# An RWKV layer with a SwiGLU block: how the receptance of chunk 1 and the keys of chunk 2 are mixed, and who makes the low parts of chunk 0

## What is computed

```python
xx = jnp.pad(x, ((0, 0), (1, 0), (0, 0)))[:, :-1]          # the step before
xk = x * time_mix_k + xx * (1.0 - time_mix_k)              # the same for xv, xr
k = jnp.einsum('btc,dc->btd', xk, Wk)                      # v and r with xv, xr
w = -jnp.exp(time_decay)
rwkv = jax.nn.sigmoid(r) * _wkv(w, time_first, k, v)
# one step of _wkv, with carries aa, bb, pp:
ww = u + kt; q = jnp.maximum(pp, ww); e1 = jnp.exp(pp - q); e2 = jnp.exp(ww - q)
y = (e1 * aa + e2 * vt) / (e1 * bb + e2)
ww2 = pp + w; q2 = jnp.maximum(ww2, kt); e1 = jnp.exp(ww2 - q2); e2 = jnp.exp(kt - q2)
aa, bb, pp = e1 * aa + e2 * vt, e1 * bb + e2, q2
# the layer:
x1 = _layernorm(x + jnp.einsum('btc,dc->btd', rwkv, Wo))
h = jax.nn.silu(x1 @ wg.T) * (x1 @ wu.T)
out = _layernorm(x1 + h @ wd.T)
```

## Time and profile before

| | us |
|---|---|
| median of 3 runs | 291.11 (290.76 to 291.33) |
| profiled execution, its time | 291.55 |
| profiled execution, span | 289.7 |
| PE busy | 273.9 (95% of the span) |
| DVE busy | 261.1 (90%) |
| ACT busy | 214.9 (74%) |
| POOL busy | 191.6 (66%) |

### The profile page before, as it was taken

One profiled execution on the slowest core, in us unless ns is written; L12 is line 12 of the kernel. 1 busy time (PEld: TensorE's weight loads), 2 busy tenths in 40 slices (PEclk: granted clock), 3 DMA queues, 4 the chain that ended last, 5 costly groups with the idle time before them and its releaser, 6 DMA issues.

```text
span 289.7 us, 4280 instructions
## 1 busy us (share of the span) xinstructions
PE 273.9 (95%) x1258; PEld 199.1 (69%) x1258; DVE 261.1 (90%) x451; ACT 214.9 (74%) x388; POOL 191.6 (66%) x155
## 2 busy tenths in 40 slices
PE   7999978889999999999999999999999999999990
PEld 5754565646794689648885679568965789778890
DVE  4996599899999999999999999999899999889773
ACT  3488797489667987699966986798858892799473
POOL 3638699979968875986768675986566580334051
PEclk9999999999999999999999999999999999999998
DMA  7900600220103102230204010210211020102003
GB/s 236 374 6 12 209 1 0 73 72 3 36 2 80 67 0 72 47 100 0 72 5 144 1 54 19 72 36 0 72 29 44 1 75 0 36 2 74 0 3 113
DMA packets 13541, 16.26 MB, mean 56 GB/s; under 512 B 720, under 2 KB 11216, under 8 KB 13520
## 3 DMA queue, kind: packets, MB, share of 16 engines
q1 hardware_dynamic: 12832, 15.48, 16.7%
q10 hardware_dynamic: 688, 0.53, 0.6%
HBM read 11.81 MB, written 4.19 MB: 55 GB/s over the span
## 4 chain that ended last, share of the span: by engine, by line
PE 72%; DVE 11%; ACT 8%; issue 4%; DMA 1%; POOL 1%; SPq 0%; DVEq 0%; POOLq 0%; ACTq 0%
PE bank_b L1163 12%; PE bank_a L1163 12%; PE bank_a L1186 11%; PE bank_b L1119 9%; PE bank_a L1082 7%; PE bank_c L1082 7%; PE bank_d L1082 7%; PE bank_b L1140 2%; DMA wkT<-wk 1%; DVE rwkv L786 1%; DVE state L746 1%; ACT L606 1%; POOL hlo L405 1%; PE bank_d L1109 1%; ACT wts L492 1%
## 5 line engine op out<-in xcount | busy, mean ns | idle before, releaser
L405 POOL TENSOR_TENSOR hlo<-hid,hhi 128x512 fp32r<-128x512 f32 (+1 forms) x37 | 54.0, 1466 | 31.7 <-ACT hhi L584 31.6
L378 POOL TENSOR_SCALAR wts<-gap,par 128x512 f32<-128x512 f32 (+1 forms) x18 | 35.9, 1995 | 24.4 <-DVE gap L714 23.5
L500 ACT ACTIVATE mix<-dx,par 128x512 f32<-128x512 f32 x48 | 31.4, 712 | 19.0 <-POOL dx L358 19.0
L1186 PE MATMUL bank_a<-wd_r,hhi 128*128 128x256 f32 x180 | 44.2, 287 | 1.0 <-POOL hlo L405 0.9
L1186 PE MATMUL bank_a<-wd_r,hlo 128*128 128x256 f32 x180 | 42.8, 279 | 0.0
L364 POOL TENSOR_TENSOR mix<-mix,xt 128x512 f32<-128x512 f32 (+1 forms) x36 | 40.7, 1164 | 0.3 <-ACT mix L500 0.3
L1186 PEld LDWEIGHTS bank_a<-wd_r,hhi 128*128 128x128 f32 x180 | 33.8, 188 | 3.5 <-issue 2.6
L1186 PEld LDWEIGHTS bank_a<-wd_r,hlo 128*128 128x128 f32 x180 | 33.8, 188 | 0.3 <-issue 0.2
L862 DVE TENSOR_TENSOR hid<-bank_b,act 128x512 f32<-128x512 f32 (+1 forms) x48 | 30.8, 643 | 3.6 <-issue 1.1
L584 ACT ACTIVATE hhi<-hid 128x512 fp32r<-128x512 f32 (+1 forms) x53 | 30.6, 579 | 4.4 <-DVE hid L862 4.4
L492 ACT ACTIVATE wts<-wts 128x512 f32<-128x512 f32 (+1 forms) x54 | 27.9, 577 | 7.5 <-DVE wts L723 7.3
(11 more groups left out here) (129 smaller groups left out, 598.1 us busy)
## 6 DMA issues: line engine op xcount, KB each, us to landing
xrow<-x SPq DMA_DIRECT2D x7, 512.0 KB, 3.8
xt<-xT SPq DMA_DIRECT2D x6, 513.0 KB, 3.7
out<-y_buf SPq DMA_DIRECT2D x6, 512.0 KB, 2.9
wg_i<-wg SPq DMA_DIRECT2D x1, 768.0 KB, 7.7
wu_i<-wu SPq DMA_DIRECT2D x1, 768.0 KB, 9.1
wd_i<-wd SPq DMA_DIRECT2D x1, 768.0 KB, 10.7
out<-y_buf SPq DMA_DIRECT2D x3, 256.0 KB, 2.2
xt<-xT SPq DMA_DIRECT2D x2, 257.0 KB, 2.9
```

The source lines that it names most:

```text
L378: nc.gpsimd.tensor_scalar(wts[:, OUT, h, 0:n], gap[:, h, 0:n], par[:, FIRST, h:h + 1], CAP, ALU.add, ALU.min).then_inc(out_arg_ready, 1)
L405: nc.gpsimd.tensor_tensor(hlo[:, m, 0:n], hid[:, m % NH, 0:n], hhi[:, m, 0:n].bitcast(f32), ALU.subtract).then_inc(hlo_ready, 1)
L500: nc.scalar.activation(mix[:, s, i, h, 0:n], dx[:, h, 0:n], ACT.Copy, scale=par[:, MIX + i, h:h + 1]).then_inc(dx_scaled, 1)
L1186: mm = nc.tensor.matmul(ffn[:, q, :], hp.bitcast(f32) if full else hp, w[:, m, :], start=(m == 0 and q % 2 == 0 and part is hhi), stop=(m ...
```

## The change

What it does, in the order of the program:

- ScalarE: the two range checks of the gate weights go ahead of an exponential and of `log_den(0)`. The by-product goes to `res2`, since `y`'s buffer now holds x of chunk 2. The scaling for R(1) is gone, and the one for K(2).
- SyncE: x of chunk 2 goes into `y`'s buffer and is loaded at once; x of chunk 3 goes to `xt` and waits for `mix_r1`; x of chunk 4 is loaded after chunk 3's mixes and stands behind the residual rows.
- VectorE: two new operations a half each, `mix_r1` (R of chunk 1, behind `x1_low(0)`) and `mix_k2` (K of chunk 2, behind `divide` of chunk 1). All of the denominator's scans of chunk 1 stand behind `mix_r1`. Low parts 4 and 5 of chunk 0 are gone.
- GpSimd: chunk 2's differences wait for `mix_r1`; half 0 of V(2) is mixed ahead of the `den` sums of chunk 1, half 1 behind them; all six low parts of chunk 0 follow in a row; the differences of chunk 3 wait for `mix_k2` and for the scaling of R(2).
- TensorE: `project_last_step(R)` is gone and R(1) is projected from its mix; the sum of the range flag stands between the halves of V(1); V(2)'s second half stands behind the whole of `down(0)`.

The diff, cut to its core:

```diff
             def load_xt(c):
-                if isinstance(c, int) and c == 2:
+                if isinstance(c, int) and c == 3:
                     sp.wait_ge(last_steps_done, 1)
-                elif isinstance(c, int) and c == 3:
-                    sp.wait_ge(squares_ready, 6)
-                elif isinstance(c, int) and c == 4:
-                    sp.wait_ge(mixed, 3 * CH)
-                elif not (isinstance(c, int) and c == 1):
+                    sp.wait_ge(r1_mixed, CH)
+                elif not (isinstance(c, int) and c < 3):
                     sp.wait_ge(mixed, (c - 2) * (3 * CH))
...
             load_xt(3)
+            load_xrow(2)
             load_xt(4)
-            load_xrow(2)
...
             def round_(j, s, ffn, ahead):
-                if not last(j):
+                if not last(j) and j > 1:
                     den_sum(j, 0)
                     den_sum(j, 1)
                 if ffn:
-                    for m in range(NP):
-                        if m == 2 and j == 1:
-                            mix_chunk(2, 0, [V])
+                    for m in range(NM if j == 1 else NP):
                         low_part(j - 1, m)
-                if j == 1:
-                    mix_chunk(2, 0, [K, R])
                 if not last(j):
                     carry_state(j + 1)
                 if ahead:
+                    if j == 1:
+                        pool.wait_ge(dx_scaled, 2 * (3 * CH))
+                        pool.wait_ge(k2_mixed, CH)
+                        diffs(3)
                     pool.wait_ge(rwkv_ready, j + 1)
-                    diffs(j + 2)
+                    if j == 1:
+                        mixing(2, 0, R, 0)
+                        mixing(2, 0, R, 1, CH + 1)
+                    else:
+                        diffs(j + 2)
                     mix_chunk(j + 2, s, [K, V] if j == 1 else range(3))
...
             pool.wait_ge(dx_scaled, 3 * CH)
-            diffs(2)
+            for h in range(CH):
+                pool.wait_ge(r1_mixed, h + 1)
+                diff(2, h)
+            mixing(2, 0, V, 0)
+            den_sum(1, 0)
+            den_sum(1, 1)
+            mixing(2, 0, V, 1)
...
-            weights(0, 1, range(2))
+            weights(0, 1, [IN_NEW])
+            range_check(0, 0)
+            weights(0, 1, [IN_OLD])
             scale_chunk(1, 1, [K])
...
             sc.preload_act_table_set("natural_log_exp_and_others")
+            range_check(0, 1)
             log_den(0)
             reciprocal(0)
-            range_check(0, 0)
-            range_check(0, 1)
-            scale_chunk(1, 1, [V])
+            scale_dx(1, 1, V, 0)
+            scale_dx(1, 1, V, 1, CH + 1)
...
             first_norm(0, True)
+            scale_dx(2, 0, V, 0)
             round_(1, 1, True, True)
...
-                    if ffn:
+                    if j > 1:
                         low_part(j - 1, NM - 2)
-                    if ffn:
                         low_part(j - 1, NM - 1)
                     divide(j)
+                    if j == 1:
+                        mix_k2(0)
+                        mix_k2(1)
...
+            def mix_r1(h):
+
+                dve.wait_ge(dx_ready, h + 1)
+                nc.vector.scalar_tensor_tensor(out=mix[:, 1, R, h, :], in0=dx[:, h, :], scalar=par[:, MIX + R, h:h + 1],
+                                               in1=xt[:, h, 0:N], op0=ALU.mult, op1=ALU.add).then_inc(r1_mixed, 1)
+
+            def mix_k2(h):
+
+                dve.wait_ge(dx_ready, CH + h + 1)
+                nc.vector.scalar_tensor_tensor(out=mix[:, 0, K, h, :], in0=dx[:, h, :], scalar=par[:, MIX + K, h:h + 1],
+                                               in1=xt2[:, h, 0:N], op0=ALU.mult, op1=ALU.add).then_inc(k2_mixed, 1)
...
                 if isinstance(j, int) and j == 1:
-                    project_change(R)
+                    project(1, 1, R)
                 gate_up(j - 1, range(2, NM), full)
...
                     down(0, range(3), full)
-                    project(2, 0, V)
+                    project(2, 0, V, [0])
                     down(0, range(3, NM), full)
+                    project(2, 0, V, [1])
...
                     project_last_step(V, [1])
-                    project_last_step(R)
+                    project_change(V, [0])
                     pe.wait_ge(out_of_range_ready, 1)
                     nc.tensor.matmul(bank_b[0:1, 1, 0:1], ones[:, :], out_of_range[:, :],
                                      start=True, stop=True).then_inc(out_of_range_total, 1)
-                    project_change(V)
+                    project_change(V, [1])
```

105 lines of the change are left out of this document (61 added, 44 removed).

## The result

| | before | after |
|---|---|---|
| median | 291.22 (290.76 to 291.65, 6 runs beside the changed kernel) | 289.07 (288.49 to 290.08, 6 runs) |
| ratio to before | | 0.993, 95% interval 0.9909 to 0.9952 |
| profiled execution, time / span | 291.55 / 289.7 | 290.07 / 288.2 |

What follows compares the result with a forecast made beforehand. TensorE was taken as the bound, with no idle time from 86 us on, so only the head could shrink, by less matmul work and fewer waits. -3.4 - 1.7 + 0.3 = -4.8 us gave a 286.3 us median; 0.80 range 285.2 to 288.8.

Steps and rivals of the forecast that it cites:

- Term 1: Head, up to the first gate matmul: removing `project_last_step(R)`'s eight passes from TensorE saves 3.4 us.
- three helpers: Range flag, `x1` and the branch on `wide` must keep pace with TensorE: zero cost taken, bound 0 to +0.5 us.
- Term 2: First gate matmul to the start of `attention_out(1)` (the mark): 20.6 us before, 18.9 after, so -1.7.
- The clock: Rival: TensorE idling about 2.2 us before `hid(3)` drops its clock to 1.2 GHz; 292.4 us, chance 0.04.
- GpSimd contended in part: Rival, before and after `attention_out(1)`: low parts at 1.3 to 1.6, mixes at 1.6; about 289.0 us, chance 0.15.
- Term 3: After `attention_out(1)`: +0.3 us, as GpSimd's `diffs(3)` wait for `mix_k2` and R(2)'s scaling; bounds 0 to +1.2.

Runs made afterwards that it cites:

- e6: Changed kernel with six matmuls of zeros in TensorE's hole and the eight passes of `project_last_step(R)` put back, result overwritten: 291.26 us, 1.0003 of the kernel before.
- e1: Changed kernel with six matmuls of zeros in TensorE's hole, ahead of chunk 0's last up tile: 288.57 us, 0.9888 of the kernel before.
- e3: Changed kernel with the mix of V(2)'s second half on GpSimd moved behind low part 1, hole not filled: 288.33 us, 0.9887 of the kernel before.
- e4: Changed kernel with six matmuls of zeros in TensorE's hole and low parts 4 and 5 back on VectorE: 287.65 us, 0.9866 of the kernel before.

## Why the prediction was wrong

**Term 1, -3.4: right.** First gate matmul 20.16 to 16.73 from the zero point, 3.43. All three helpers kept pace: the flag's matmul at 25.08 within V's, no wait at the branch, transposes at 27.02. e6 shows it twice, at the gate and at the mark. It is the whole gain of this change: e6, with all the rest and the clock whole, is where the kernel before is.

**Term 2, -1.7: wrong; measured +2.5.** The forecast for the mark was 35.61 from the zero point and it came at 39.81, 4.20 later. In the profiled executions that splits into 1.75 (35.61 to 37.36, e1) and 2.45 (37.36 to 39.81).

- *The step that failed first is the price of GpSimd's sum ahead of the low parts and of VectorE's scans beside it.* It took the differences at 1.0 and the first mix at 1.15, from rows in which VectorE did other work, and gave VectorE the mean of all scans. The change puts just these beside each other. On GpSimd: differences +1.33, first mix +1.04, second mix +0.7 over the 1.35 used, less 0.64 as it began earlier; so low part 0 came 2.24 late from the zero point (28.80 for 26.56). On VectorE: `hid(0)` 0.3 late, the numerator's scans +1.0, so `num_new` ended 1.35 after what mean scans gave; then 0.45 of waiting. `hid(3)` was 2.2 late (29.65 for 27.46). The larger part came by VectorE: in e3, where low part 0 was out of the way, `hid(3)` was still 1.65 late (29.11), and only 0.54 was the wait for GpSimd's queue. The row that could have told it was there: the `den` sums' 3.26 for two, which I called contended and did not carry over to the operations next to them.
- *Behind `hid(3)` the sum had slack that the kernel doesn't have.* I let the low parts set the end. From the start of `hid(3)` to the mark it has 8.15; e1 took 7.72 (42.41 to 50.13), of which 7.23 are TensorE's own work with hardly a gap. So of the 2.19 that `hid(3)` was late 1.75 went to the mark.
- *The clock.* I named the place and the hole and gave it 0.04, since no row showed the clock fall for so short a pause. It fell. Its price in the rival, 6.2 us, was too high: the clock was back at 47.5, so only part of down(0) and V(2) ran at 1.2 GHz. 2.45 us were lost in the profiled execution, by the medians 0.5 to 1.6.
- *The rival "GpSimd contended in part"* gives nearly the right time, about 289.0, but for another reason: it had low parts at 1.3 to 1.6. They took 1.02 each; ahead of them and beside the clock lay what was missing.
- `mix_r1`, 0.7 each: measured 1.41 for two. R(1) was not waited for. VectorE's terms up to `num_new` add up to 39.7 as written, not 39.5; each start lies some 0.08 ahead of the end before it, which covers it. `divide`: 1.23, forecast 1.2. Moving low parts 4 and 5 took 2.72 us off VectorE, as said, but e4 shows that nothing was won by it. The mix of K(2) on VectorE was not tried alone.

**Term 3, +0.3: no such loss is seen.** Mark to the end of the span is 237.33 before and 237.15 after, -0.18, just under the lower bound of 0; but this stretch varies by 1.0 between the kernels here, so neither 0.3 nor -0.18 can be told from zero. Chunk 3's differences at 48.85, the output argument of chunk 2 at 60.11, 9.06 after the mark, and the transposes wait 0.29 for x1.

**The balance.** Mark 47.25 forecast and 51.05 measured, +3.80 (4.20 less 0.40 for the earlier zero point); behind the mark 239.0 for 239.5; so the profiled execution took 290.07 for 286.75. The median lies 1.0 below that execution, where I had put 0.44. Had all executions lost what the profiled one did, the miss in the median would have been larger.

## What to carry to other kernels

When a change lays GpSimd and VectorE side by side where they were apart, price both at rows in which such operations overlap, above all where the sum of one of them gates the other; here it turned a gain of 1.7 us into none. A forecast that contains an idle piece of TensorE in the midst of matmuls has to carry the clock's fall as a main case, and a few matmuls of zeros in that piece, or an order that shortens it, settle it cheaply; whether the clock fell is to be read from the granted clock of every execution, not of the profiled one alone. A move that relieves an engine is worth something only where that engine's work ends last: two of this change's moves, undone one at a time, changed the mark by under 0.2.
